# Graph layer: loads reordered over two queues, weights turned first, PSUM copies ahead of VectorE waits, decodings spread, bias additions between the first gathers

## What is computed

```python
xn = layernorm(x)
x = x + gnn(xn, edges, Wq, bq, Wk, bk, Wv, bv, Wo, bo) + mix(xn, w_qkv, mem_kv, w_out, b_out, g_out, g_pre)
x = x + ffn(layernorm(x), gate_w, gate_b, w1, b1, w2, b2)
# gnn: q, k, v = xn @ W.T + b (8 heads of 32); per edge sim = q[dst] . k[src] / sqrt(32);
#      softmax of sim over the edges of one dst; agg = sum of attn * v[src]; agg @ Wo.T + bo
# mix: rmsnorm(xn) @ w_qkv; q softmaxed over features, k over nodes (4 memory columns added);
#      context = k v^T; out = q context; rmsnorm(out @ w_out + b_out) + xn
# ffn: top-1 routing to 8 experts of 489 places, relu(h @ w1 + b1) @ w2 + b2
```

## Time and profile before

| what | us |
|---|---|
| median of 3 runs | 1391.93 (1388.9 to 1399.45) |
| the profiled execution | 1398.41 |
| its span | 1396.6 |
| TensorE, VectorE, ScalarE, GpSimd busy | 994.1, 879.1, 479.5, 561.3 |
| mean granted clock of TensorE | 0.821 of full |

### The profile page before, as it was taken

The page is one execution under the profiler, slowest core; times in us unless marked ns, Lnnn a source line. Parts: engine busy times, 40 slices in busy tenths (PEclk is TensorE's granted clock), DMA queues, the critical chain, the costliest instruction groups (busy, mean ns, idle before and its releaser), DMA issues. The chain is left out here.

```text
span 1396.6 us, 17914 instructions
## 1 busy us (share of the span) xinstructions
PE 994.1 (71%) x4183; PEld 687.1 (49%) x4184; DVE 879.1 (63%) x1736; ACT 479.5 (34%) x1320; POOL 561.3 (40%) x629
## 2 busy tenths in 40 slices
PE   1899636657577666777667566657768839999996
PEld 1455423445444444555445444435545835666764
DVE  2679628668677776777767767767867342433543
ACT  2465425334233332334333333323432402222121
POOL 1516265346545555455644444554410012232221
PEclk9999768778868887787877878877789558999998
DMA  4242360456656566566665655556402350443220
GB/s 153 83 102 72 107 190 15 121 138 175 178 159 169 151 181 165 158 168 161 175 173 151 160 139 158 158 161 174 123 1 102 121 194 27 141 148 100 100 98 7
DMA packets 82665, 183.55 MB, mean 131 GB/s; under 512 B 11862, under 2 KB 46476, under 8 KB 82629
## 3 DMA queue, kind: packets, MB, share of 16 engines
q0 software_dynamic: 39488, 126.26, 33.4%
q1 hardware_dynamic: 40297, 54.53, 12.0%
q10 hardware_dynamic: 2844, 2.35, 0.6%
HBM read 166.03 MB, written 20.85 MB: 134 GB/s over the span
## 5 line engine op out<-in xcount | busy, mean ns | idle before, releaser
L886 POOL DMA_INDIRECT slot<-kv_d,idx x408 | 389.6, 955 | 367.1 <-DVE at_pv L991 253.0
L1124 PE MATMUL at_pa<-at_pv,at_hot 128*125 128x264 f32 x880 | 302.9, 489 | 210.9 <-DVE agg L1005 106.0
L1124 PEld LDWEIGHTS at_pa<-at_pv,at_hot 128*125 128x125 f32 x880 | 192.8, 237 | 293.3 <-issue 148.2
L1114 PE MATMUL at_pq<-q,at_hotT 125*128 x1320 | 206.0, 323 | 10.9 <-POOL at_sign L874 6.7
L975 DVE TENSOR_TENSOR at_prod<-at_pq,slot 128x1024 f32<-128x1024 f32 x110 | 133.9, 1217 | 82.5 <-remote 61.8
L1114 PEld LDWEIGHTS at_pq<-q,at_hotT 125*128 125x128 bf16 x1320 | 147.8, 115 | 57.3 <-issue 18.4
L1005 DVE TENSOR_TENSOR agg<-agg,at_pa 125x264 f32 x220 | 92.8, 422 | 104.7 <-remote 88.8
L910 ACT ACTIVATE at_hot<-at_habs,one_col 128x500 f32<-128x500 f32 x110 | 78.3, 712 | 199.6 <-remote 98.7
L991 DVE TENSOR_TENSOR at_pv<-slot,at_pp 128x1056 f32<-128x1056 f32 x110 | 136.7, 1243 | 3.9 <-PE at_pp L1147 2.1
L906 ACT ACTIVATE at_habs<-iota_w,nloc_e 128x125 f32<-128x125 f32 x440 | 138.2, 384 | 0.1
L982 DVE TENSOR_REDUCE at_sc<-at_prod 128x32 f32<-128x1024 f32 x110 | 133.4, 1213 | 2.0
(11 more groups left out here) (289 smaller groups left out, 1305.2 us busy)
## 6 DMA issues: line engine op xcount, KB each, us to landing
slot<-in_w SPq DMA_DIRECT2D x16, 1024.0 KB
locrow<-loc_d SPq DMA_DIRECT2D x28, 500.0 KB
slot<-kv_d,idx POOLq DMA_INDIRECT x408
kv_d<-vst SPq DMA_DIRECT2D x25, 128.9 KB
base<-in_x SPq DMA_DIRECT2D x5, 625.0 KB
kv_d<-kst SPq DMA_DIRECT2D x25, 125.0 KB
row_d<-base SPq DMA_DIRECT2D x5, 625.0 KB
out<-base SPq DMA_DIRECT2D x5, 625.0 KB
```

Source lines behind the costliest of these rows:

```text
L886: pool.indirect_dma_start(slot[par][:, u, :], None, m.kv_d, bass.IndirectOffsetOnAxis(ap=m.idx[:, par, u:u + 1].bitcast(U32), axis=0)).the ...
L1114: mm = pe.matmul(pq[q % 2][:, u * D:(u + 1) * D], hotT[:, 4 * q + u, :], at(m.q3, wins[u // 2])[:, part, :], start=(part == 0), stop=(part ...
L1124: mm = pe.matmul(pa[p % 2][:, 0:H * VW], hot[:, u % 8, :], pv[:, u % 8, :, :].rearrange("p h c -> p (h c)"), start=(u % 2 == 0), stop=(u % ...
```

## The change

Six edits:

1. SP reads `last_i` before it loads the second group of x. The biases and the loads for linear attention move from ScalarE's queue to SP's: the biases behind the second group of x, the others behind the last. `bo` gets a buffer of its own, which lives through linear attention.
2. TensorE turns the weights before it sums the rows of edges. VectorE scales `w_qkv` before it looks for the rows, and takes the statistics of the second group after that. ScalarE copies the weights before it squares the first tiles, and has `xnT` of tiles 0 and 1 ready before the loop.
3. In the loop ScalarE first copies `pc` of tile t, then `xnT` of tile t + 2, and only then does what waits for VectorE.
4. The decodings move from tiles 1 and 2 to tiles 4 and 6, `columns` from 5 and 7 to 8 and 10, `negated` from 16 to 14; SP's stores and reads of the keys move two tiles on. The flags (`marked`) are made at tile 16 and the comparisons (`compared`) at the last four tiles instead of behind the loop.
5. GpSimd's key subtractions move from tiles 13 to 22 to tiles 19 to 22.
6. GpSimd's additions of `bo` move out of the loop of `prepare`: in `linear_attention` one stands behind each of the first 25 gathers.

```diff
@@ sync @@
-                nodes(1)
                 sp.wait_ge(S.edges_in, 96)
                 sp.dma_start(last_i[:, :, :], m.edges.rearrange("(g p) c -> p g c", p=RP)).then_inc(S.last_in, 16)
+                nodes(1)
+                for i, b in enumerate((io.bq, io.bk, io.bv)):
+                    sp.dma_start(m.bqkv[:, i * D:(i + 1) * D], b.partition_broadcast(TT)).then_inc(S.b_in, 16)
+                sp.dma_start(m.bo[:, :], io.bo.partition_broadcast(TT)).then_inc(S.bo_in, 16)
                 for g in range(2, NT // LG):
                     nodes(g)
+                mem = io.mem_kv.rearrange("a h d m -> a (h d) m")
+                sp.dma_start(m.mk[:, :], mem[0]).then_inc(S.mem_in, 16)
...
-                for t in range(5):
+                for t in range(7):
                     stored(t)
                 sp.wait_ge(S.keys_made, TG)
...
-                for t in range(7, NT):
-                    if t < 7 + H:
-                        h = t - 7
+                for t in range(9, NT):
+                    if t < 9 + H:
+                        h = t - 9
@@ gpsimd, prepare @@
-                pool.wait_ge(S.bo_in, 16)
                 for t in range(NT):
                     pool.wait_ge(S.xn_made, t + 1)
                     pool.tensor_tensor(m.base[:, t, :], m.base[:, t, :], m.xn[:, t, :], ALU.add).then_inc(S.base_x, 1)
-                    pool.wait_ge(S.base_x, t + 1)
-                    pool.tensor_tensor(m.base[:, t, :], m.base[:, t, :], bo[:, :], ALU.add)
-                    if t == 13:
-                        pool.wait_ge(S.key_in, 16 * H + 16)
-                    if t >= 13 and (t - 13) % 3 == 0:
-                        c = slice((t - 13) // 3 * 7, ((t - 13) // 3 + 1) * 7)
+                    if t >= NT - 6 and t < NT - 2:
+                        if t == NT - 6:
+                            pool.wait_ge(S.key_in, 16 * H + 16)
+                        c = slice((t - NT + 6) * 7, (t - NT + 7) * 7)
@@ vector, prepare @@
+                def compared(i):
+                    c = slice(7 * i, 7 * i + 7)
+                    dve.wait_ge(S.borders_made, i + 1)
+                    dve.tensor_scalar(m.edge[:, c, :], m.edge[:, c, :], 0.0, -RESET, ALU.not_equal, ALU.mult)
+
+                def marked():
+                    dve.wait_ge(S.key_in, 16 * H + 16)
+                    dve.wait_ge(S.flags_clear, 1)
...
                 for t in range(NT):
                     projected(t)
-                    if t == 1:
+                    if t == 0:
+                        offsets(1)
+                    if t == 4:
                         decoded(0)
-                    if t == 2:
+                    if t == 6:
                         decoded(1)
-                    if t == 5:
+                    if t == 8:
                         columns(0)
-                    if t == 7:
+                    if t == 10:
                         columns(1)
+                    if t == 14:
+                        negated()
                     if t == 16:
-                        negated()
+                        marked()
+                    if t >= NT - 4:
+                        compared(t - NT + 4)
@@ gpsimd, linear_attention @@
-                gather_chunk(pool, m, 0, m.slot0, 0, U)
-                pool.wait_ge(S.ctx_made, 1)
-                pool.nop(nofuse=True)
-                gather_chunk(pool, m, 1, m.slot1, 0, U)
+                pool.wait_ge(S.bo_in, 16)
+                for u in range(2 * U):
+                    if u == U:
+                        pool.wait_ge(S.ctx_made, 1)
+                        pool.nop(nofuse=True)
+                    gather_chunk(pool, m, u // U, (m.slot0, m.slot1)[u // U], u % U, u % U + 1)
+                    if u < NT:
+                        pool.tensor_tensor(m.base[:, u, :], m.base[:, u, :], m.bo[:, :], ALU.add).then_inc(S.base_x, 1)
+                pool.wait_ge(S.base_x, 2 * NT)
                 add_mixed(pool, m, 0, SOON)
```

More of the change, by code:

```diff
@@ L238, in _ @@
                 sp.dma_start(m.loc[0:STEPS, :].rearrange("(g p s) e -> p g (s e)", p=TP, s=2), loc16[:, :, :]).then_inc(S.keys_out, 16)
-                for t in range(5, 7):
+                for t in range(7, 9):
                     stored(t)
@@ L416, in _ @@
                                       ALU.mult).then_inc(S.w_ready, 1)
+                rows_found()
+                rows_numbered()
+                bounded(0)
+                inverted(0)
+                measured(1)
                 dve.wait_ge(S.b_in, 48)
@@ L496, in _ @@
                     normalised(t)
-                for t in range(LG):
-                    squares(t)
-                rooted(1)
                 for w in range(4):
@@ L505, in _ @@
                 turn_out(0)
+                for t in range(LG):
+                    squares(t)
+                turn_out(1)
                 norms(0)
-                normalised(LG)
-                squares(LG)
                 for t in range(NT):
                     par = t % 2
-                    if t + 1 < NT:
-                        turn_out(t + 1)
-                    if t > 0:
-                        second(t - 1)
                     act.wait_ge(S.projected, t + 1)
@@ L533, in _ @@
             def _(pe):
-                pe.wait_ge(S.before_made, RG)
-                for j in range(TG):
-                    for g in range(RG):
-                        pe.matmul(ptab[0:TP, j:j + 1], before[:, g, j * TP:(j + 1) * TP], ones[:, 0:1], start=(g == 0), stop=(g == RG - 1))
-                for g in range(RG):
-                    last = pe.matmul(ptab[0:2, 8:8 + PAIRS], ones[:, :], before[:, g, :], start=(g == 0), stop=(g == RG - 1))
-                last.then_inc(S.rows_counted, 1)
                 pe.wait_ge(S.ident_made, 1)
@@ L566, in _ @@
                 turn_in(0)
+                pe.wait_ge(S.before_made, RG)
+                for j in range(TG):
+                    for g in range(RG):
+                        pe.matmul(ptab[0:TP, j:j + 1], before[:, g, j * TP:(j + 1) * TP], ones[:, 0:1], start=(g == 0), stop=(g == RG - 1))
+                for g in range(RG):
+                    last = pe.matmul(ptab[0:2, 8:8 + PAIRS], ones[:, :], before[:, g, :], start=(g == 0), stop=(g == RG - 1))
+                last.then_inc(S.rows_counted, 1)
                 pe.wait_ge(S.w_evac, 4)
```

51 lines of the change are left out of this document (22 added, 29 removed).

## The result

The changed kernel took 1418.12 us (median of 4, 1411.36 to 1421.68); the kernel before, run beside it, 1395.69 us (median of 4, 1388.9 to 1414.97). The ratio is 1.0171, 95% interval 1.0102 to 1.0241: in this pair slower by 1 to 2.4%, where 1374.6 us was forecast. The profiled execution took 1421.68 us, span 1419.9.

The account below looks back on a forecast made before the run. TensorE was taken to bound the tile loop; gains 3.9 + 10.0 + 1.4 + 2.0 = 17.3 us turned the profiled 1398.4 into 1381.1 and the median 1391.9 into 1374.6 us. Range 1363 to 1387, the forecast's own 1368 to 1381.

Parts of the forecast that it names:

- The start: Before and into `prepare`'s tile loop: TensorE's fifth tile done at 56.7 instead of 60.56, gain 3.9 us, bounds 0 and 7.4.
- the loads end at 44 to 46 as before: SP's queue: reordered loads still end at 44 to 46 us, so tile 0's store lands at 48.5 (46 to 51).
- The stalls in the loop: `prepare`'s tile loop: TensorE's two stalls, 11.0 us with slow clock, go; gain 10.0 us, bounds 4.8 and 11.0.
- the end of `prepare`: Behind the tile loop: flags and comparisons move into it, leaving SP's last store late; gain 1.4 us (0.5 to 2.5).
- I leave 1.0 us: Tile 16 of `prepare`'s loop: 1.0 us allowed for `marked()` waiting for the last keys and making VectorE late.
- Both stalls go: TensorE's stalls at 64.27 and 137.57 vanish, since VectorE is at most 2.0 us behind against a cover of 3.0.
- Linear attention: Linear-attention stage: `bo` additions among the gathers, 66.6 us against 69.0; gain 2.0 us, bounds 3.8 and -10.4.
- the fourth rival: Linear attention: additions and VectorE block each other, gather-addition pairs grow from 2.04 to 3.2 us; 1403.2 us, chance 0.05.
- what makes room for it: Linear attention: VectorE's waits beside back-to-back gathers, 7.45 us and two of about 6, vanish when gathers are spaced.
- The remaining 1165 us of the span are work that the change does not touch.: Everything after linear attention, from 231.69 us on: 1165 us unaffected, so every term lies in the first 231.69 us.
- the third: Start of `prepare`: edge table near 27, store near 51, so the 3.9 us gain is lost; 1378.5 us, chance 0.10.
- VectorE stays late in the loop: Tile loop: one 6.2 us stall stays and linear attention gains nothing; 1382.8 us, second rival, chance 0.20.

Follow-up runs that it names:

- a_stores: Changed kernel, SP's queue reordered: last two x groups and five linear-attention loads moved behind first stores; 1211.68 us where an attention chunk takes 22 us.
- a_best: Changed kernel with SP's last x groups and linear-attention loads behind first stores, and `bo` additions back in `prepare`'s loop; 1199.63 us, ratio 0.9903 to the kernel before.
- after_again: The changed kernel as it is, run again on a chip of the faster kind; 1226.27 us, ratio 1.0136 to the kernel before.
- after_third: The changed kernel as it is, repeated once more on a chip where a chunk takes 22 us; 1225.23 us, ratio 1.0125 to the kernel before.
- before_prof: The kernel before, unchanged, profiled for its stages on a chip where a chunk takes 22 us; 1214.07 us (one execution).
- b_weigh: Kernel before with VectorE's weighing of a chunk's last quarter moved ahead of the product that needs the next rows; 1219.07 us (one execution), faster kind of chip.
- b_spaced: Kernel before with only the 25 `bo` additions moved from `prepare`'s loop to between the first gathers; median 1402.32 us, ratio 0.9941 to the kernel before.
- b_spaced_2: Kernel before with only the 25 `bo` additions moved between the first gathers, run again where a chunk takes 22 us; 1218.75 us (one execution).
- a_prep: Changed kernel with the `bo` additions back in `prepare`'s loop; 1408.33 us, ratio 1.0058 to the kernel before; repeated where a chunk takes 22 us: 1207.62 us, 0.997.
- a_pace: Changed kernel with SP's queue reordered, `bo` additions back in `prepare`, and eight empty GpSimd instructions behind each attention-loop gather; ratio 0.9923 to the kernel before.
- a_pace_2: Repeat, where a chunk takes 30 us: changed kernel, SP's queue reordered, `bo` additions back in `prepare`, eight empty GpSimd instructions per attention-loop gather; 1393.56 us, ratio 0.9942.

## Why the prediction was wrong

The profile is 40.6 us above the 1381.1 that the sum gave for it (1421.68). 12.0 of these lie ahead of attention, where 17.3 was forecast and 5.3 came: that is where the steps below failed. The other 28.8 lie in a loop that the change does not touch, and the later runs make its spread the likeliest cause: bad luck, for which the prediction had no allowance. Without it the forecast would still have been 12 us off on this chip, and on a chip of the other kind the sign would have been wrong all the same.

**The start (3.9 us, bounds 0 and 7.4): wrong, -2.4.** The mechanism was the right one: loads fill the queue, the first stores stand behind them, and VectorE's tile 2 waits. The loop's start came out (23.02, forecast 23.5), although x landed at 13.51 and not at 12.0: the 23.5 stood on the edge table, which came at 18.30 where 18.8 to 21 was forecast, so the error on x stayed hidden; that part of the agreement is luck. Wrong was "the loads end at 44 to 46 as before" as the time of the store: I took a rate of bytes and left out that issuing takes the queue's own time, which the trace before showed (16.73 and 6.73 us), and that five loads and the second x group with four biases now stand in between. The store went out at 48.6 to 48.95 and VectorE went on at 55.05, 6.1 us after the issue, where I had 3.6; the fifth tile started at 56.19 instead of 49.7. That is 6.5 us, and the bound of 0 ("store no earlier than before") did not think of a later one. The orders of a_stores and a_best show the price: 6 to 9 us of `prepare`'s end.

**The stalls in the loop and the end of `prepare` (10.0 and 1.4): 6.7 together.** From the fifth tile's end to the stage's end it was 102.1 us before (162.68 - 60.56), now 95.4 (158.38 - 62.99); the loop gave 5.7 of it and the end 1.0. The failed step here is "I leave 1.0 us" for `marked()`. TensorE's stall of 2.67 at 126.26, with slow products behind it (3.30 us, where an undisturbed tile of this timeline has 1.88), is that wait; the tile took 8.72 us instead of 4.09. VectorE's rows:

```profile
119.98 0.62 DVE L403 TENSOR_TENSOR flags<-slot 1x448 bf16<-1x448 f32 x1 [2.17 <-DMA slot<-key_d]
120.63 1.70 DVE L405 TENSOR_SCALAR flags<-flags 1x448 bf16<-1x448 bf16 x1
122.36 1.00 DVE L403 TENSOR_TENSOR flags<-slot 1x448 bf16<-1x448 f32 x1
123.39 1.70 DVE L405 TENSOR_SCALAR flags<-flags 1x448 bf16<-1x448 bf16 x1
```

The wait was 2.17 us where I had about 1, and the work 5.1 us (119.98 to 125.09) where I had 1.7: it ran beside GpSimd's four key subtractions, released by the same load. In the kernel before, without GpSimd beside it, the whole took 1.96 us, and the operation of 1.70 us took 0.32.

"Both stalls go" held for the two old ones; this one is new, and so is a third that the prediction had no term for. At 86.02 TensorE waits 2.04 us to turn the second half of the edge tables: it needs VectorE to have copied the first half out (`columns(0)`), which now stands at tile 8 behind a group's statistics, just where the prediction had VectorE 2.0 us behind. The tile took 6.70 us where the one with the first half took 4.47, so 2.2 are lost; in after_again and after_third the wait is 2.7 us and two tiles take 7.36 and 5.78, some 4.5 lost.

Last, 4.7 of the 11.0 for the old stalls was slow clock behind them (2.99 and 1.71), and that is not a fixed price. The same stall of 3.0 to 3.1 us near the loop's end is followed by a tile of 5.80 us at a granted clock of 0.71 in the kernel before, of 7.09 at 0.57 in before_prof and of 4.11 at 1.00 in b_weigh, all with the same code.

Also left without a term was what GpSimd's additions cost the old order, though their share was named (L403's 0.685 us); b_spaced and b_spaced_2 take them out of `prepare`, which ends 5.7 and 5.9 us earlier (156.95 and 155.44 against 162.68 and 161.36). Against the 158.26 of b_weigh it would be 1.3 to 2.8, so the size is uncertain. In the changed order they cost nothing: a_prep, with them back, ends `prepare` at 156.08 and 157.98, against 158.38 and 158.30.

**Linear attention (2.0 us, bounds 3.8 and -10.4): 1.0 on the first chip, -16 on others.** The stage came out at 67.97, forecast 66.6, with GpSimd the bound and VectorE's longest wait 2.3 us instead of 7.45, as worked; a pair took mostly 1.87 us, never 2.75, so the fourth rival did not come. But the term rested on "what makes room for it": standstills that belong to the chip of the first profile. Where gathers back to back cause none, the 16.8 us of GpSimd are paid nearly in full. Nothing in one profile shows that; the bound of -10.4 stood for dearer additions, not for the loss of the cover.

**"The remaining 1165 us of the span are work that the change does not touch."** True of the code, false of the time: in the first pair the loop moved by 28.8 us. The last paragraph of the prediction says that I had no term for it, and the range of the three executions shown (1388.9 to 1399.45) hid a spread of 50 us. On a chip of the first kind no difference is shown: 1.7% slower in the first pair, equal medians in the larger batch (1405.42 and 1407.09). On one of the second kind the change is 1.25 to 1.4% slower, which is the 16 us of linear attention; what `prepare` gains there (158.30 and 159.40 against 161.36) is within its own spread.

Of the rivals, the third, a start without its gain, happened in its outcome: the edge table was in time, the store was later still than its 51. "VectorE stays late in the loop" happened too, as two waits of 2.04 and 2.67 us with slow products behind the second, instead of one of 6.2.

## What to carry to other kernels

Before work is put into an engine's gaps, ask what makes the gaps: a gap that ends with a late semaphore of a DMA can be absent on another chip, and then the filler is the bound. Stores that release a double buffer belong in a queue ahead of loads that are needed later; read the issue durations of the queue, not only the bytes. Before a difference of 1 to 2% is explained, compare the stages that the change did not touch: if they move by more than those it did, repeat the pair.

## What the runs showed of the hardware

- Two kinds of chips in these runs: the kernel before takes 1395 to 1410 us on one (three batches of runs) and 1210 to 1211 on the other (three), with equal busy time of VectorE, ScalarE and GpSimd. Stretches of before_prof, linear attention and attention, to be read against the earlier trace rows and the 805.49 us above:

```profile
161.36:213.38 52.02, 34.23 (x136) 22.32 (x136) 38.19 (x84) 26.02 (x86) 38.66 (x44) 0.76 0.63 174
213.38:852.97 639.59, 482.69 (x2480) 348.42 (x2480) 580.41 (x914) 296.60 (x834) 401.62 (x431) 0.89 0.69 192
```

  Only the two stretches with gathers back to back differ: linear attention (52.0 and 69.0) and attention (640 and 805), not `prepare` (161.4 and 162.7), nor what follows (359.3 and 359.4). With additions between the gathers linear attention takes 68 us on both. TensorE is busy 54 us longer in attention on the first kind, at a mean granted clock of 0.78 instead of 0.89; it also idles longer there, 268.6 us against 156.9.
- The issue of a DMA behind large loads is not free: 17.49 us for three loads of 625 KB, 5.32 us for one of 2 KB behind them; 16.73 and 6.73 us in the kernel before.
- What a stall of 3 us of TensorE costs in clock varies with the same code: the tile behind it took 4.11, 5.80 or 7.09 us, at a granted clock of 1.00, 0.71 and 0.57.
- A small VectorE operation (448 elements of one partition) took 1.70 us beside GpSimd's key subtractions and 0.32 us alone.
- Eight empty instructions on GpSimd between two gathers cost nothing in a_pace: the gap stays at 0.30 us.
- a_best, the changed kernel with both corrections, is the fastest found: 0.9903 and 0.9904 of the kernel before where a chunk takes 22 us; in the form a_pace_2, 0.9942 where it takes 30.
